# Attention's key and query loads: 12 transfers a tile with a repeated source, in place of 20

## The chip, the cores and the metric

The kernel is one program on one core of a Trainium2 chip. The metric is the device time of one execution in microseconds (us); less is better. Matmuls run on TensorE (PE in the profile, its weight loads PEld), the rest on VectorE (DVE), ScalarE (ACT) and GpSimd (POOL). The SyncE sequencer (SP) only issues transfers and waits. A transfer (DMA) can be issued by SP, ACT or POOL; its bytes are moved by the core's 16 DMA engines, in packets.

## The reference

Two transformer-like layers over a batch of 4 sequences of 512 rows of 256 numbers, all in float32. The part that the change touches is the causal attention of the first layer, with 16 heads of 16 numbers each:

```python
Q = split_heads(Xn @ Wq + bq)
K = split_heads(Xn @ Wk + bk)
V = split_heads(Xn @ Wv + bv)
scores = jnp.einsum('bhqd,bhkd->bhqk', Q, K) / jnp.sqrt(jnp.float32(D_HEAD))
scores = jnp.where(causal, scores, jnp.float32(-jnp.inf))
A = jax.nn.softmax(scores, axis=-1)
AV = jnp.einsum('bhqk,bhkd->bhqd', A, V)
return AV @ Wo + bo
```

After it come a mixture of 16 experts, a gated convolution with an MLP, and a mixture of 2 experts. None of them is touched.

## The kernel before

The program is a row of stages, each a block in which every engine has its own instruction stream, with semaphores between the streams and a barrier of all engines at each block's end.

**The projection stage** (`attention_inputs`) computes queries, keys and values for the four sequences b = 0 to 3 in a software pipeline (`wavefront`). Each float32 number is split into a high and a low part that TensorE can multiply exactly (`qhi` and `qlo`; names with k_parts, q_parts and v_parts are scratch tensors in device memory). SP stores the results with `store(b)`: for each b eight transfers of 256 KB at L212 (four to q_parts, four to k_parts) and one of 1 MB to v_parts at L216. The source of an L212 store is a tile of 128 partitions; its destination is seen as 8 blocks of 16 rows of 512 numbers, because the two parts of one head lie behind each other. ACT evicts the projections (L327), and in `first_keys` it also issues the very first key and query loads of attention, since SP is busy storing: half of them at b = 2 and half at b = 3. POOL makes `qlo` (L259), then the low part of V, and last stores five small row sets (L272, mod_rows), for whose arrival SP waits (L223) before the stage can end.

**The attention stage** (`attention`) works through 16 tiles, called quads below: 4 sequences times 4 groups of 4 heads. Its loop does two quads, u = 0 and u = 1, per turn (8 turns, a pair of quads each), and each has its own buffers: K4_0 and Q4_0, K4_1 and Q4_1. For head s of a quad, partitions 64·(s % 2) to 64·(s % 2) + 63 of the buffer hold the products' factors in this order: keys hi, lo, hi, lo against queries hi, lo, lo, hi, so that one matmul adds all four products. So every row is needed twice, and `load_keys` fetches it twice from device memory: for each head two transfers of 32 partitions for the keys (L560), one of 32 for the queries (L562) and two of 16 (L564). That is 20 transfers a quad. A row is 512 numbers, 2 KB.

PE computes the scores of a head (L660 with the mask at L661), DVE takes their maxima (L758), ACT the exponentials (L717), POOL scales (L635), PE transposes (L673), ACT and DVE split again (L727, L766), PE multiplies by V (L689), four heads behind the scores. SP's order in one turn of the loop, from `pair`: wait until the scores of quad u = 0 are done, then load_keys for the next quad in those buffers; the same for u = 1; wait until the values of u = 0 are done, then four loads of V (L568); the same for u = 1. PE waits at a quad's first matmul for all its K and Q transfers (`k_in`, `q_in`), and at its first value matmul for V.

Of the kernel before, what the change touches and what calls it, by code (L numbers as in the profile page):

```python
# [16 lines left out]
B, T = 4, 512  # L17
NT = B * T // P
TT = T // P
HEADS, DH = 16, 16  # L20
# [20 lines left out]
def f32(ap):  # L41

    return ap.bitcast(F32)
# [7 lines left out]
def wait(eng, sem, n):  # L51

    if not isinstance(n, int) or n > 0:
        eng.wait_ge(sem, n)

def wavefront(*stages):

    for step in range(B + max(lag for lag, _ in stages)):
        for lag, stage in stages:
            if 0 <= step - lag < B:  # L60
                stage(step - lag)
# [70 lines left out]
def attention_inputs(k, heads, x, cT, wmod, w, ln_gb, bqk, bv_row):  # L132
# [5 lines left out]
    with ExitStack() as c:  # L138
# [135 lines left out]
        @block.scalar  # L274
        def _(act):
            act.wait_ge(c_in, 16)
            act.activation(scT[:], cs[:], ACT.Silu).then_inc(silu_done, 1)

            def evict(b):

                if b < 2:
                    for i in (FIRST_LAYER[1:], SECOND_LAYER)[b]:
                        act.wait_ge(row_ready, i + 1)
                        act.activation(row[:, i, :], k.PS[0:B, 2 + i, :], ACT.Copy).then_inc(evicted, 1)
                    act.wait_ge(cols_ready, b + 1)
                    first, last = COL_PARTS[b][0], COL_PARTS[b][-1]
                    act.activation(k.modc[:, b, first:last + 1].rearrange("p c m b -> p (c m b)"),
                                   cols[:, b, DM * first:DM * (last + 1)].rearrange("p j b -> p (j b)"), ACT.Copy).then_inc(evicted, 1)

            def weights(b):  # L290
                if b == 0:
                    act.wait_ge(w_in, 48)
                    act.activation(whi[:], wst[:], ACT.Copy).then_inc(w_hi, 1)
                    act.wait_ge(par_in, 48)
                    act.mul(bq[:, 0], bq[:, 0], 0.25).then_inc(bq_done, 1)
                    act.wait_ge(bq_done, 1)

            def normalize(i, src, out, free, done):

                def stage(b):  # L300
                    act.wait_ge(nb_ready[i], b + 1)
                    free(b)
                    for t in range(TT):
                        act.activation(out(b, t), src(b, t), ACT.Identity, scale=rs[:, i, b, t:t + 1],
                                       bias=nb[:, i, b, t:t + 1]).then_inc(done, 1)
                return stage
            first_norm = normalize(0, lambda b, t: k.X[:, b * TT + t, :], lambda b, t: xh[:, b % 2, t, :],
                                   lambda b: wait(act, xh_used, b - 1), xh_done)
            second_norm = normalize(1, lambda b, t: h[:, b % 2, t, :], lambda b, t: hn[:, t, :],
                                    lambda b: wait(act, hT_ready, b * DM), hn_ready)  # L310

            def columns(b):

                if b >= 2:
                    act.wait_ge(v_ready, (b - 1) * 2)
                for m in range(DM):
                    act.wait_ge(hf_done, b * DM + m + 1)
                    act.activation(hhi[:, b % 2, m, :], k.PS[:, m, :], ACT.Identity, scale=gb[:, 0, m:m + 1],
                                   bias=gb[:, 1, m:m + 1]).then_inc(hhi_done, 1)

            def queries(j):
                def stage(b):
                    act.wait_ge(q_ready, b * 4 + j + 1)
                    if b:
                        act.wait_ge(q_out[j], b * 32)
                    for out in (qf[:, j, :], qhi[:, j, :]):
                        act.activation(out, k.PS[:, 2 + j, :], ACT.Identity, scale=(0.25 if j < 2 else 1.0),  # L327
                                       bias=bq[:, j // 2, j % 2:j % 2 + 1]).then_inc(q_done, 1)
                return stage

            def values(b):
                if b:
                    act.wait_ge(v_out, b * 16)
                for g in range(2):
                    act.wait_ge(vf_done, b * 2 + g + 1)
                    for t in (2 * g, 2 * g + 1):
                        last = act.activation(vp[:, t, :, 0, :], vf[:, t, :].rearrange("p (h d) -> p h d", d=DH), ACT.Copy)
                    last.then_inc(vhi_done, 1)

            def first_keys(b):  # L340

                if b >= 2:
                    act.wait_ge(heads.zeroed, 4)
                    heads.wait_stored(act, 0)
                    heads.load_keys(act, 0, 0, 0, range(2 * b - 4, 2 * b - 2))
            wavefront((2, columns), (3, queries(0)), (3, queries(1)), (3, queries(2)), (0, first_norm), (0, evict), (1, weights), (1, second_norm),
                      (3, queries(3)), (3, values), (3, first_keys))

        @block.vector
# [180 lines left out]
class Heads:  # L530
# [20 lines left out]
            pool.memset(f32(self.K4[u][:]), 0.0).then_inc(self.zeroed, 1)  # L551
            pool.memset(f32(self.V4[u][:]), 0.0).then_inc(self.zeroed, 1)

    def load_keys(self, sp, b, q, u, heads=range(4)):

        for s in heads:
            r = 64 * (s % 2)
            src = self.k.k_parts[b, q, s].rearrange("a r t -> (a r) t")
            for dup in range(2):
                sp.dma_start(f32(self.K4[u][r + 32 * dup:r + 32 * dup + 32, s, :]), src).then_inc(self.k_in[u], 16)  # L560
            src = self.k.q_parts[b, q, s]
            sp.dma_start(f32(self.Q4[u][r:r + 32, s // 2, :]), src.rearrange("a r t -> (a r) t")).then_inc(self.q_in[u], 16)  # L562
            for dup in range(2):
                sp.dma_start(f32(self.Q4[u][r + 32 + 16 * dup:r + 48 + 16 * dup, s // 2, :]), src[1 - dup]).then_inc(self.q_in[u], 16)  # L564

    def load_values(self, sp, b, q, u):
        for s in range(4):
# [14 lines left out]
def attention(k, heads, OT, out_weights, wo):  # L582
# [3 lines left out]
    with ExitStack() as c:  # L586
        Q4, K4, V4, k_in, q_in, v_in = heads.Q4, heads.K4, heads.V4, heads.k_in, heads.q_in, heads.v_in
# [58 lines left out]
        def _(pe):  # L646
            def body(it, on):
                for e in range(8):
                    h = it * 8 + e

                    def scores(i):
                        u, s = e // 4, e % 4
                        if s == 0 and i == 0:

                            pe.wait_ge(k_in[u], it * 128 + 128)
                            pe.wait_ge(q_in[u], it * 192 + 192)
                        w = P * (i + 1)

                        wait(pe, exp_done, (h - 1) * TT + i + 1)
                        pe.matmul(k.PS[:, i, 0:w], Q4[u][:, s // 2, P * i:P * i + P], K4[u][:, s, 0:w], start=True, stop=False)  # L660
                        pe.matmul(k.PS[:, i, w - P:w], k.identb[:], k.maskb[:], start=False, stop=True).then_inc(s_ready, 1)  # L661
# [31 lines left out]
                    if on(e, 0):  # L693
                        for i in range(TT - 1):
                            scores(i)
                    if on(e, VALUES):
                        values()
                    if on(e, 0):
                        scores(TT - 1)
# [1841 lines left out]
```

## Time and profile before

| | |
|---|---|
| median of 3 runs | 1178.86 us (1175.69 to 1179.64) |
| the profiled execution | 1173.97 us, span 1171.9 us |
| granted TensorE clock, mean over the span | 0.90 of full speed |
| PE busy | 954.3 us, 81% of the span |
| DVE, ACT, POOL busy | 742.1, 652.3, 456.9 us |
| attention stage, first score to last value | 118.4 to 362.2 us |
| bytes moved by DMA | 123.15 MB, mean 105 GB/s |

Times in a trace count from the start of the span. A timeline row gives start, duration, engine and line; a row with SPq, ACTq or POOLq is the issuing of a transfer by that sequencer, and its duration is how long the sequencer was held, not how long the bytes took. "To landing" is the time from issue to the last byte. The DMA share of a window is the mean busy share of the 16 DMA engines: 0.50 can be all of them half the time, or eight of them all the time.

### The profile page before, as it was taken

How to read it: one execution, taken by the hardware profiler on the slowest of the kernel's cores; microseconds unless marked ns; L12 is line 12 of the kernel's file. 1: busy time of each engine (PE TensorE's matmuls, PEld its weight loads, DVE VectorE, ACT ScalarE, POOL GpSimd, SP SyncE). 2: the span in 40 equal slices, each digit the busy share in tenths (PEclk: the TensorE clock that was granted, in tenths of full speed). 3: DMA queues.
4: the chain of work that ended last, by engine and by line, in shares of the span. 5: the costliest groups of instructions: out<-in, count | busy, mean ns of one | idle time of the engine just before them, and what ended most of it. 6: DMA issues, size and time to landing. Idle time of an engine off the chain costs nothing. (4 is left out here: it accounts for less than half of the span.)

```text
span 1171.9 us, 21496 instructions
## 1 busy us (share of the span) xinstructions
PE 954.3 (81%) x5454; PEld 796.3 (68%) x5454; DVE 742.1 (63%) x1917; ACT 652.3 (56%) x1693; POOL 456.9 (39%) x637
## 2 busy tenths in 40 slices
PE   6671999999997767969999970689699974999992
PEld 2461788888886655758999960468487753888882
DVE  4870798999994676468555535996447773444444
ACT  3562898999993345458666642579533322333331
POOL 3373564666662177603444443576301121010000
PEclk9786898999998787979999995799899986999997
DMA  7066443343322522447343429310042203000004
GB/s 247 17 222 212 114 102 90 91 90 90 90 54 64 180 100 101 153 150 251 124 128 121 126 98 303 99 45 1 14 143 75 72 28 127 24 31 33 28 15 152
DMA packets 112107, 123.15 MB, mean 105 GB/s; under 512 B 46720, under 2 KB 85120, under 8 KB 111896
## 3 DMA queue, kind: packets, MB, share of 16 engines
q1 hardware_dynamic: 102584, 97.89, 28.4%
q0 software_dynamic: 8608, 23.20, 5.3%
q10 hardware_dynamic: 832, 1.05, 0.3%
q8 instruction: 40, 0.66, 0.2%
q14 instruction: 43, 0.35, 0.1%
HBM read 77.73 MB, written 44.35 MB: 104 GB/s over the span
## 5 line engine op out<-in xcount | busy, mean ns | idle before, releaser
L717 ACT ACTIVATE PR<-PS,nmax 128x128 f32<-128x128 f32 (+3 forms) x256 | 135.7, 553 | 9.7 <-DVE nmax L758 8.4
L758 DVE TENSOR_REDUCE nmax<-PS 128x1 f32<-128x128 f32 (+3 forms) x256 | 113.5, 481 | 42.4 <-PE PS L661 37.0
L635 POOL TENSOR_SCALAR PR<-PR,rinv 128x128 f32<-128x128 f32 (+3 forms) x256 | 132.3, 537 | 0.0
L1355 POOL DMA_INDIRECT r_results<-r_y,r_to x79 | 75.9, 961 | 111.8 <-DVE r_to L1410 76.8
L660 PE MATMUL PS<-K,Q 128*128 128x128 f32 (+3 forms) x256 | 84.6, 390 | 30.4 <-PEq L138 26.4
L766 DVE TENSOR_TENSOR PTlo<-PS,PThi 128x512 fp32r<-128x512 f32 (+1 forms) x192 | 103.0, 590 | 2.9 <-ACT PThi L727 2.9
L727 ACT ACTIVATE PThi<-PS 128x512 fp32r<-128x512 f32 (+1 forms) x192 | 97.0, 547 | 6.7 <-PE PS L673 6.7
L673 PE MATMUL PS<-ident,PR 128*128 128x128 f32 x640 | 86.7, 281 | 3.6 <-DVE PTlo L766 3.0
L689 PE MATMUL PS<-PThi,V 128*128 128x512 f32 (+3 forms) x256 | 85.3, 346 | 1.1 <-DVE PTlo L766 0.5
L2350 DVE TENSOR_TENSOR x_h<-PS,x_sg 128x256 f32<-128x256 f32 x68 | 28.9, 424 | 86.4 <-ACT x_sg L2304 86.4
L2304 ACT ACTIVATE x_sg<-PS 128x256 f32<-128x256 f32 x68 | 26.2, 385 | 95.2 <-PE PS L2444 95.2
L2279 POOL DMA_INDIRECT x_results<-x_y,x_to x17 | 16.4, 963 | 156.2 <-DVE x_to L2345 143.8
L689 PE MATMUL PS<-PTlo,V 128*128 128x512 f32 (+3 forms) x256 | 76.2, 323 | 0.0
L673 PEld LDWEIGHTS PS<-ident,PR 128*128 128x128 f32 x640 | 69.6, 143 | 9.6 <-DVE PTlo L766 5.5
L949 POOL DMA_INDIRECT r_sorted<-o_hrow,o_slots x64 | 64.8, 1012 | 28.7 <-issue 18.7
L1399 DVE TENSOR_TENSOR r_xlo<-PS,r_xhi 128x256 fp32r<-128x256 f32 x79 | 33.4, 423 | 65.6 <-ACT r_xhi L1370 61.2
L660 PEld LDWEIGHTS PS<-K,Q 128*128 128x128 f32 x256 | 51.7, 206 | 32.8 <-issue 30.0
L2442 PE MATMUL PS<-r_wlo,r_xhi 128*128 x158 | 59.7, 378 | 2.5 <-issue 2.0
L1370 ACT ACTIVATE r_xhi<-PS 128x256 fp32r<-128x256 f32 x79 | 30.4, 385 | 56.1 <-PE PS L2444 54.0
L661 PE MATMUL PS<-maskb,identb 128*128 128x128 bf16 x256 | 60.8, 238 | 0.0
L717 ACT ACTIVATION_READ_ACCUMULATOR PR<-PS,nmax 128x1 f32 x256 | 58.7, 229 | 0.0
L2428 PE MATMUL PS<-x_w,x_hhi 128*128 (+1 forms) x136 | 57.2, 437 | 1.8 <-DVE x_hlo L2354 1.7
(374 smaller groups left out, 3067.8 us busy)
## 6 DMA issues: line engine op xcount, KB each, us to landing
r_xg<-r_sorted SPq DMA_DIRECT2D x79, 129.0 KB
r_wst<-in_routed SPq DMA_DIRECT2D x16, 608.0 KB, 5.3
K<-k_parts SPq DMA_DIRECT2D x120, 64.0 KB, 1.8
v_parts<-vp SPq DMA_DIRECT2D x4, 1024.0 KB, 7.5
V<-v_parts SPq DMA_DIRECT2D x64, 64.0 KB, 2.1
mlp_st<-r_results SPq DMA_DIRECT2D x8, 512.0 KB, 7.9
c_yg<-r_results SPq DMA_DIRECT2D x8, 512.0 KB
mlp_st<-in_up SPq DMA_DIRECT2D x8, 512.0 KB, 3.7
```

The costliest lines, as they stand in the source:

```text
L635: pool.tensor_scalar(PR[:, e % 4, i, 0:w], PR[:, e % 4, i, 0:w], rinv[:, e % 4, i:i + 1], 1.0, ALU.mult, ALU.mult).then_inc(norm_done, 1)
L660: pe.matmul(k.PS[:, i, 0:w], Q4[u][:, s // 2, P * i:P * i + P], K4[u][:, s, 0:w], start=True, stop=False)
L661: pe.matmul(k.PS[:, i, w - P:w], k.identb[:], k.maskb[:], start=False, stop=True).then_inc(s_ready, 1)
L673: ins = pe.transpose(k.PS[:, 4 + bank, at % 512:at % 512 + P], PR[:, (e - TRANS) % 4, i, P * j:P * j + P], k.ident[:])
L689: ins = pe.matmul(O[:, P * j:T], V4[u][:, j, s, :], pt[:, ge % 2, PT_AT[j]:PT_AT[j] + w], start=(s == 0 and j == 0 and part == 0), stop=(s ...
L717: act.activation(PR[:, e % 4, i, 0:w], k.PS[:, i, 0:w], ACT.Exp, bias=nmax[:, e % 4, i:i + 1], accum_out=rsum[:, e % 4, i:i + 1]).then_inc ...
L727: act.activation(PThi[:, e % 2, at:at + w], k.PS[:, 4 + n, 0:w], ACT.Copy).then_inc(hi_done, 1)
L758: dve.tensor_reduce(nmax[:, e % 4, i:i + 1], k.PS[:, i, 0:P * (i + 1)], AX_X, ALU.max, negate=True).then_inc(max_done, 1)
L766: dve.tensor_tensor(PTlo[:, (e - LO) % 2, at:at + w], k.PS[:, 4 + n, 0:w], f32(PThi[:, (e - LO) % 2, at:at + w]), ALU.subtract).then_inc(l ...
L949: pool.indirect_dma_start(out=d.sorted, out_offset=bass.IndirectOffsetOnAxis(ap=slots[:, b * TT + t, choice:choice + 1], axis=0), in_=hrow ...
L1355: pool.indirect_dma_start(out=d.results, out_offset=bass.IndirectOffsetOnAxis(ap=to[:, i % TO_LANES:i % TO_LANES + 1], axis=0), in_=y[:, i ...
L2442: pe.matmul(out, x_hi, w_lo, start=first, stop=False)
```

## The change

```diff
             def first_keys(b):
 
-                if b >= 2:
+                if b == 2:
                     act.wait_ge(heads.zeroed, 4)
                     heads.wait_stored(act, 0)
-                    heads.load_keys(act, 0, 0, 0, range(2 * b - 4, 2 * b - 2))
+                    heads.load_keys(act, 0, 0, 0)
...
-    def load_keys(self, sp, b, q, u, heads=range(4)):
-
-        for s in heads:
+    def load_keys(self, sp, b, q, u):
+
+
+        for s in range(4):
             r = 64 * (s % 2)
-            src = self.k.k_parts[b, q, s].rearrange("a r t -> (a r) t")
-            for dup in range(2):
-                sp.dma_start(f32(self.K4[u][r + 32 * dup:r + 32 * dup + 32, s, :]), src).then_inc(self.k_in[u], 16)
-            src = self.k.q_parts[b, q, s]
-            sp.dma_start(f32(self.Q4[u][r:r + 32, s // 2, :]), src.rearrange("a r t -> (a r) t")).then_inc(self.q_in[u], 16)
-            for dup in range(2):
-                sp.dma_start(f32(self.Q4[u][r + 32 + 16 * dup:r + 48 + 16 * dup, s // 2, :]), src[1 - dup]).then_inc(self.q_in[u], 16)
+            for a in range(2):
+                src = self.k.k_parts[b, q, s, a].unsqueeze(0).to_broadcast([2, DH, T])
+                sp.dma_start(f32(self.K4[u][r + 32 * a:r + 32 * a + 32, s, :]), src).then_inc(self.k_in[u], 16)
+            src = self.k.q_parts[b, q, s].rearrange("a r t -> (a r) t").unsqueeze(0).to_broadcast([2, 2 * DH, T])
+            sp.dma_start(f32(self.Q4[u][r:r + 64, s // 2, :]), src).then_inc(self.q_in[u], 16)
...
-                            pe.wait_ge(q_in[u], it * 192 + 192)
+                            pe.wait_ge(q_in[u], it * 64 + 64)
```

The keys now lie hi, hi, lo, lo and the queries hi, lo, hi, lo, which gives the same four products. A key transfer takes one part (16 rows) with its source repeated twice, in steps of (2, 16, 512) with a step of zero for the 2; a query transfer takes both parts (32 rows), repeated twice, in steps of (2, 32, 512). The bytes and the 2 KB rows moved are the same: 512 rows, 1 MB, a quad. A quad has 8 key transfers of 64 KB and 4 query transfers of 128 KB, 12 in place of 20.

On SP, at the start of the attention stage, the second quad's keys and queries and the first two quads' values stand like this before the change (shapes are those of the destination; the number behind a name is the buffer u):

```order
L560 DMA K4_1<-k_parts 32x512 x2
L562 DMA Q4_1<-q_parts 32x512
L564 DMA Q4_1<-q_parts 16x512 x2
L560 DMA K4_1<-k_parts 32x512 x2
L562 DMA Q4_1<-q_parts 32x512
L564 DMA Q4_1<-q_parts 16x512 x2
L568 DMA V4_0<-v_parts 128x4x32 x4
L568 DMA V4_1<-v_parts 128x4x32 x4
```

These are its last two heads of four; the first two read alike. After the change the same place reads:

```order
L561 DMA K4_1<-k_parts 32x1x512 x2
L563 DMA Q4_1<-q_parts 64x1x512
L561 DMA K4_1<-k_parts 32x1x512 x2
L563 DMA Q4_1<-q_parts 64x1x512
L567 DMA V4_0<-v_parts 128x4x32 x4
L567 DMA V4_1<-v_parts 128x4x32 x4
```

The place in SP's order is the same; three issues a head stand where five stood.

On ACT, in the projection stage, the loads for the first quad stood in two batches, one behind the evictions of b = 2 and one behind those of b = 3 (L327 are evictions of queries and keys, L337 of values):

```order
L337 ACTIVATE vp<-vf 128x16x16 x4
L560 DMA K4_0<-k_parts 32x512 x2
L562 DMA Q4_0<-q_parts 32x512
L564 DMA Q4_0<-q_parts 16x512 x2
L560 DMA K4_0<-k_parts 32x512 x2
L562 DMA Q4_0<-q_parts 32x512
L564 DMA Q4_0<-q_parts 16x512 x2
L327 ACTIVATE qf<-PS,bq 128x512
```

Now all twelve stand in front of the evictions of b = 3:

```order
L337 ACTIVATE vp<-vf 128x16x16 x4
L561 DMA K4_0<-k_parts 32x1x512 x2
L563 DMA Q4_0<-q_parts 64x1x512
L561 DMA K4_0<-k_parts 32x1x512 x2
L563 DMA Q4_0<-q_parts 64x1x512
L561 DMA K4_0<-k_parts 32x1x512 x2
L563 DMA Q4_0<-q_parts 64x1x512
L561 DMA K4_0<-k_parts 32x1x512 x2
L563 DMA Q4_0<-q_parts 64x1x512
L327 ACTIVATE qf<-PS,bq 128x512
```

Ten transfers stood ahead of these evictions before, twelve do now, and the ten behind them are gone. The order of the other engines is unchanged.

## Rows read from the trace of the kernel before

**Rows 1.** The page's first line.

```profile
span 1171.9 us, 21496 instructions
```

**Rows 2.** Windows: first quad, fifth quad, quads 7 to 15.

```profile
core 0: us, PE busy (x) PEld busy (x) DVE busy (x) ACT busy (x) POOL busy (x), PEclk, DMA share, GB/s
118.37:131.29 12.92, 11.59 (x52) 8.77 (x53) 8.76 (x22) 11.03 (x35) 4.66 (x12) 0.61 0.47 119
177.09:193.53 16.44, 16.44 (x105) 14.39 (x105) 13.04 (x32) 12.19 (x39) 6.88 (x17) 0.82 0.32 76
208.30:337.21 128.91, 127.49 (x937) 109.66 (x937) 124.26 (x298) 124.65 (x404) 79.99 (x180) 1.00 0.39 91
```

**Rows 3.** Waits of PE, 131 to 355 us: total, times, longest.

```profile
PE PS L660 <- DMA Q<-q_parts: 2.9, 1, 2.9
```

**Rows 4.** Timeline of PE: first score of quads 7 and 16.

```profile
208.30 0.32 PE L660 MATMUL PS<-K,Q 128*128 128x128 f32 x1 [0.15 <-ACT PR L717]
...
337.21 0.31 PE L660 MATMUL PS<-K,Q 128*128 128x128 f32 x1
```

**Rows 5.** DMA issues by tile: count, KB each, median us to landing.

```profile
K<-k_parts SPq DMA_DIRECT2D x120, 64.0 KB, 1.8
...
V<-v_parts SPq DMA_DIRECT2D x64, 64.0 KB, 2.1
...
Q<-q_parts SPq DMA_DIRECT2D x60, 64.0 KB
Q<-q_parts SPq DMA_DIRECT2D x120, 32.0 KB
```

**Rows 6.** Windows in the projection stage: L212 stores alone, then the v_parts store.

```profile
73.00:76.80 3.80, 0.74 (x6) 0.74 (x7) 3.51 (x6) 1.29 (x4) 1.37 (x2) 1.00 0.53 198
96.00:98.00 2.00, 0.00 (x0) 0.00 (x0) 0.00 (x0) 0.00 (x0) 0.00 (x0) 0.50 1.01 329
```

**Rows 7.** DMA, 72 to 76.5 us: queue (packets, MB, share), then issues.

```profile
q1 hardware_dynamic: 450, 0.87, 52.7%
...
k_parts<-qhi SPq DMA_DIRECT2D x2, 256.0 KB
k_parts<-qlo SPq DMA_DIRECT2D x2, 256.0 KB
```

**Rows 8.** Timeline of SP: two L212 stores.

```profile
68.44 0.61 SPq L212 DMA_DIRECT2D q_parts<-qhi  x1
...
73.02 1.31 SPq L212 DMA_DIRECT2D k_parts<-qlo  x1
```

**Rows 9.** Timeline of ACT: its loads behind b = 2, and what follows.

```profile
84.75 0.40 ACTq L560 DMA_DIRECT2D K<-k_parts  x1
...
96.22 3.07 ACTq L564 DMA_DIRECT2D Q<-q_parts  x2
99.40 0.69 ACT L327 ACTIVATE qf<-PS,bq 128x512 f32<-128x512 f32 x1 [13.39 <-issue]
```

**Rows 10.** Timeline of POOL: the row sets' issue; their landing.

```profile
108.40 2.85 POOL L272 DMA_DIRECT2D mod_rows<-row  x5
...
DMA to landing us min/median/max: 5.5/6.8/6.9
```

**Rows 11.** Timeline of SP: values, then output weights.

```profile
128.53 5.51 SPq L568 DMA_DIRECT2D V<-v_parts  x8
...
160.67 4.73 SPq L579 DMA_DIRECT2D wo_st<-in_wo  x8
```

**Rows 12.** DMA queue, 129.5 to 134.5 us (values), 161 to 166 us (output weights).

```profile
q1 hardware_dynamic: 3696, 0.46, 59.4%
...
q1 hardware_dynamic: 1324, 0.55, 49.0%
```

## The prediction

> **What bounds the kernel now.** I started from the page's first line, the span of 1171.9 us [rows 1], and cut it at the attention stage, the only long stage that the change touches. In its steady part PE is busy 127.5 of 128.9 us at full clock (the third window of [rows 2]). From quad 7's first score to quad 16's are 337.21 - 208.30 = 128.9 us, nine quads of 14.3 us each [rows 4]. The reader is to see that PE, with DVE and ACT right behind it at 124 us, sets the pace, and that the DMA engines stand at a share of 0.39 and 91 GB/s. Then I read PE's waits in this stage. Transfers of K and Q held it up once, for 2.9 us, at quad 5, where the loads of the output weights had put SP behind [rows 3]. So the key and query loads are hidden, and fewer issues have nothing to shorten here. The question is whether the loads stay hidden.
>
> **How a transfer's shape sets its speed.** I then looked at the stores of the projection stage, since there transfers queue up and the engines' limit shows. The L212 stores read 128 partitions and write 8 blocks of 16 rows. While they alone are under way, the 16 DMA engines show a share of 0.53 and 198 GB/s (the first window of [rows 6]; [rows 7] shows that nothing else was issued). This is no lack of work: SP is held 1.31 us by one such store, where an earlier one with a free queue took 0.61 us [rows 8]. The v_parts store, whose outermost step counts 128 on both sides, reaches a share of 1.01 and 329 GB/s (the second window of [rows 6]). I read this so: a transfer is cut along the outermost step of its access on both sides, and the side with the fewer steps limits how many engines work on it. Eight blocks give eight engines, and always the same eight, or the next store in the queue would have filled the others. One engine then moves 198 / 8 = 24.8 GB/s, a 2 KB row in 83 ns.
>
> The old key and query transfers are flat: 32 or 16 rows on both sides, so 16 engines with one or two rows each. The new sources begin with the repetition, an outermost step of 2. By the same reading each new transfer goes over two engines, and all of them over the same two.
>
> The page "DMA: Bandwidth & Descriptors" of the Trainium skill says this outright (Rules for kernel authors, "Use all 16 engines"): an outermost dimension of size c below 16, a leading zero-stride broadcast among its examples, confines the whole DMA to at most c engines. By that rule the eight-block stores should show a share of 0.50; the trace agrees, with 0.53. The same section has a rule for the change: coalesce many small transfers, since those under 64 KB are mostly overhead. By it the time would fall or stay, and the trace is against that having anything to give, as the wait of 2.9 us says.
>
> **The change in the attention stage.** A quad's keys and queries are 8 x 64 + 4 x 64 + 8 x 32 = 1024 KB before (the counts of [rows 5] over 15 quads) and as many after: 1.049 MB / (2 x 24.8 GB/s) = **21.2 us** on the two engines, against 14.3 us of computing. The eight value loads of a pair of quads lie in the same queue. They keep an engine busy 59.4% of 5 us = 3.0 us at least [rows 12], and SP's issuing takes 5.5 us at most [rows 11]; I take the middle, 4.3 us. So a pair of quads needs 2 x 21.2 + 4.3 = **46.7 us**, where it took 28.6 us. The queue is rarely empty: the next loads into buffer 0 may start once the scores of quad u = 0 are done, which is 21.2 + 1 + 14.3 = 36.5 us into the period of 46.7 us, and those into buffer 1 about 11 us in, when the queue gets to them at 21.2 us. The cover is 10 us both times. TensorE's clock does not change that. Waiting PE will be at half clock more often, but the fifth quad, at a mean of 0.82, took 16.4 us (the second window of [rows 2]). That is 2.1 us more for (1 - 0.82) x 2 x 16.4 = 5.9 us at half clock, so about 14.3 + 5.1 = 19.4 us for a quad at half clock throughout, within the cover. The 8 issues a quad that are saved are worth nothing against this, nor is the wait of 2.9 us that goes with them.
>
> **The change in the projection stage.** ACT's ten loads took from 84.75 to 99.3 us to issue, at about 1.45 us each, because SP's stores were queued; the evictions of b = 3 waited 13.4 us behind them [rows 9]. From their start at 99.4 us the rest of the chain follows: POOL's work, its row sets from 108.4 us (2.85 us to issue, 6.8 us to land [rows 10]), and the end of the stage at about 118.2 us, 18.8 us later. After the change the two engines have, from 84 us on, SP's 13 remaining L212 stores (16 rows per engine each), two v_parts stores (32 each) and the first quad's 256: 208 + 64 + 256 = 528 rows, 528 x 83 ns = 43.8 us, so until 127.8 us. The evictions start when most of ACT's 256 and SP's 112 rows of b = 2 are through, at about 110 us, which also gives 110 + 19 = 129 us. I take **129 us** for the start of attention. The ends: 118.2 us if the queues swallow all without holding ACT, 134 us if ACT is held to its last row.
>
> **The sum.** Quad 2's loads and the first values: 129 + 21.2 + 4.3 = 154.5 us. Seven pairs of 46.7 us: 481.4 us. The output weights, once, between 2.5 us (49% of 5 us [rows 12]) and 4.7 us [rows 11], say 3.0: 484.4 us. The last values come behind the last keys: - 4.3. One us for landing (a key load takes 1.8 us from issue to landing with nothing ahead [rows 5]): quad 16 starts at 481.1 us, where it started at 337.2 us [rows 4]: + 143.9 us. The last quad and the tail begin at less than full clock, between 0 and 5 us, I take 2. In all **+146 us**. The profiled execution took 1173.97 us, so 1320 us; on the median of 1178.86 us it would be 1325 us. I give **1318 us**, a shade under both, since 198 GB/s is the slowest I saw eight engines run when full and has a moment of slack in it. Nothing behind attention is changed.
>
> The ends of the unknown costs: start at 118.2 us, values 3.0 us, weights 2.5 us, no tail give 1297 us, and engines 5% faster take another 16 us off, 1281 us. Each engine at 329 / 16 = 20.6 GB/s, as in the v_parts store, with every other term at its high end, would be 25.5 us a quad and about 1400 us; but there all 16 were drawing on device memory at once, two will not. One engine at 22.8 GB/s, halfway, gives about 1350 us.
>
> **The rivals.** *All 16 engines serve the new transfers anyway* (chance 0.10): the eight blocks are on the written side and come from distinct rows, and a repeated read may be cut differently. Then the loads stay hidden, SP issues 8 transfers a quad less, PE's 2.9 us at quad 5 go, and ACT's twelve issues in place of ten ahead of the evictions cost 2 x 1.45 = 2.9 us: between 1170 and 1177 us on the profiled time, no change. This is the case on the other side, not slower. It decides from four engines on: 10.6 us of loads and 2.2 of values are then under the 14.3 us of a quad. The rule to coalesce belongs here, with a chance of a third of it for a gain over the bound. *Two engines each, but others from transfer to transfer* (0.04): SP would issue faster than two engines move, and eight pairs would work side by side; same time as the first rival. Against it stands the half share under a full queue. *Four engines or so* (0.04), if the inner step of 16 or 32 takes part: hidden in attention, a few us lost in the projection stage, 1180 to 1190 us. The forecast, two fixed engines, has 0.82.
>
> **How the numbers follow.** A difference of 0.3%, 3.5 us, is about what a measurement of this kernel can tell from none. Faster: 0.03, a third of the first rival. Same: the rest of it and the second, 0.11. Slower: 0.82 + 0.04 = 0.86. The range is the forecast's own, 1280 to 1350 us; the other cases, 0.18 in all, lie below it.
>
> **What would show it.** If right: in the steady part of attention the DMA share is about 2/16 = 0.13 plus a little for the values, with 60 GB/s or less; K and Q loads land many us after issue in place of 1.8; SP is held over 1 us by an issue where it took 0.37; PE's first score of each quad waits about 9 us for K or Q; quads start every 23.4 us; the clock falls in the waits; POOL's L272 issues at about 119 us. It is wrong if key loads still land in 2 to 3 us with a share near 0.4, or if PE's waits sit elsewhere.

## The result, and the profile after

The changed kernel takes 1340.2 us (median of 4 runs, 1337.11 to 1340.75) against 1177.28 us before: the ratio is 1.1382, with a 95% interval of 1.1344 to 1.142. That is 163 us more, where 139 were forecast (1318 us, range 1280 to 1350).

The page of the changed kernel, its first line and three of its lists (compare [rows 1] and [rows 5]; the queue row gives packets, MB and share):

```profile
span 1338.7 us, 21262 instructions
...
q1 hardware_dynamic: 98144, 97.87, 23.8%
...
L659 PE MATMUL PS<-K,Q 128*128 128x128 f32 (+3 forms) x256 | 95.7, 432 | 165.6 <-DMA Q<-q_parts 113.7
...
K<-k_parts SPq DMA_DIRECT2D x120, 64.0 KB
Q<-q_parts SPq DMA_DIRECT2D x60, 128.0 KB
V<-v_parts SPq DMA_DIRECT2D x64, 64.0 KB, 2.2
```

Queue 1 moves the 97.9 MB that it moved before, but PE's score matmuls at L659 (L660 before) now have 165.6 us of idle time in front of them, 113.7 of it put down to the query loads.

PE's waits in the changed kernel, 131 to 513 us (compare [rows 3]):

```profile
PE PS L659 <- DMA Q<-q_parts: 113.7, 14, 14.9
PE PS L659 <- issue: 13.7, 1, 13.7
```

One wait of 2.9 us has become a wait at every quad. The same place by windows: nine quads of the steady part, and ten of its microseconds in which only key and query rows are moved (compare [rows 2]):

```profile
core 0: us, PE busy (x) PEld busy (x) DVE busy (x) ACT busy (x) POOL busy (x), PEclk, DMA share, GB/s
283.47:498.27 214.80, 146.67 (x936) 126.44 (x937) 128.33 (x297) 130.44 (x405) 79.88 (x180) 0.80 0.19 55
335.00:345.00 10.00, 10.00 (x77) 8.87 (x76) 8.90 (x22) 8.13 (x26) 5.61 (x14) 0.97 0.13 49
```

Nine quads take 214.8 us in place of 128.9. The reader is to see the second window: a DMA share of 0.13, with 49 GB/s. Sixteen times 0.13 is two engines, busy all the time. This is no idle queue, as the timeline of SP shows in the same stretch:

```profile
331.35 3.66 SPq L561 DMA_DIRECT2D K<-k_parts  x2
335.14 1.12 SPq L563 DMA_DIRECT2D Q<-q_parts  x1
336.56 4.13 SPq L561 DMA_DIRECT2D K<-k_parts  x2
340.79 1.16 SPq L563 DMA_DIRECT2D Q<-q_parts  x1
342.14 5.14 SPq L567 DMA_DIRECT2D V<-v_parts  x2
```

SP is held in its issues, and so are the two value loads behind them, 2.6 us each, though they go over all engines. Over all 64 value loads of each kernel (ns min/median/max; L568 is before, L567 after):

```profile
L568 SPq DMA_DIRECT2D V<-v_parts x64: 368/373/1732, 128.5 to 337.9; - x64
L567 SPq DMA_DIRECT2D V<-v_parts x64: 372/1606/2607, 145.7 to 499.1; - x64
```

The projection stage, ACT and POOL (compare [rows 9, 10]), and the first scores of quads 1, 2 and 16 (compare [rows 4]):

```profile
92.28 7.22 ACTq L561 DMA_DIRECT2D K<-k_parts  x2
...
108.84 1.24 ACTq L563 DMA_DIRECT2D Q<-q_parts  x1
110.20 0.69 ACT L327 ACTIVATE qf<-PS,bq 128x512 f32<-128x512 f32 x1 [23.57 <-issue]
...
119.20 2.85 POOL L272 DMA_DIRECT2D mod_rows<-row  x5
...
129.95 0.44 PE L659 MATMUL PS<-K,Q 128*128 128x128 f32 x1 [37.77 <-PEq L138]
...
157.10 0.44 PE L659 MATMUL PS<-K,Q 128*128 128x128 f32 x1 [13.74 <-issue]
...
498.27 0.47 PE L659 MATMUL PS<-K,Q 128*128 128x128 f32 x1 [5.10 <-DMA Q<-q_parts]
```

The evictions of b = 3 begin at 110.2 us, where they began at 99.4, and attention at 129.95 us, where it began at 118.4. Quad 16 begins 161.1 us later than before.

### The profile page after: what moved, and what is told of

Its sections match the earlier page's. It is cut to its first block and busy times, and to the rows that moved or that the text cites. A ratio compares the mean times of both kernels' runs of the same rounds, so it can differ in the third digit from the quotient of the medians.

```text
span 1338.7 us, 21262 instructions
## 1 busy us (share of the span) xinstructions
PE 985.6 (74%) x5454; PEld 822.7 (61%) x5454; DVE 747.2 (56%) x1917; ACT 659.6 (49%) x1693; POOL 456.0 (34%) x637
## 3 DMA queue, kind: packets, MB, share of 16 engines
q10 hardware_dynamic: 536, 1.05, 0.2%
## 5 line engine op out<-in xcount | busy, mean ns | idle before, releaser
L757 DVE TENSOR_REDUCE nmax<-PS 128x1 f32<-128x128 f32 (+3 forms) x256 | 118.1, 485 | 199.0 <-PE PS L660 193.2
L659 PE MATMUL PS<-K,Q 128*128 128x128 f32 (+3 forms) x256 | 95.7, 432 | 165.6 <-DMA Q<-q_parts 113.7
L659 PEld LDWEIGHTS PS<-K,Q 128*128 128x128 f32 x256 | 59.4, 235 | 169.8 <-issue 169.1
L631 POOL TENSOR_TENSOR carry<-rinv 128x1 f32<-128x1 f32 x64 | 12.4, 193 | 255.9 <-DVE rinv L783 255.8
L688 PE MATMUL PS<-PThi,V 128*128 128x512 f32 (+3 forms) x256 | 96.2, 386 | 1.0 <-DVE PTlo L765 0.5
L688 PE MATMUL PS<-PTlo,V 128*128 128x512 f32 (+3 forms) x256 | 85.7, 360 | 0.0
L672 PEld LDWEIGHTS PS<-ident,PR 128*128 128x128 f32 x640 | 74.8, 151 | 4.6 <-issue 0.9
L660 PE MATMUL PS<-maskb,identb 128*128 128x128 bf16 x256 | 65.9, 258 | 0.0
L688 PEld LDWEIGHTS PS<-PThi,V 128*128 128x128 f32 x256 | 57.6, 225 | 5.0 <-DVE PTlo L765 0.7
L688 PEld LDWEIGHTS PS<-PTlo,V 128*128 128x128 f32 x256 | 56.8, 222 | 3.5
```

Of the source, the lines that this page charges most:

```text
L672: ins = pe.transpose(k.PS[:, 4 + bank, at % 512:at % 512 + P], PR[:, (e - TRANS) % 4, i, P * j:P * j + P], k.ident[:])
L688: ins = pe.matmul(O[:, P * j:T], V4[u][:, j, s, :], pt[:, ge % 2, PT_AT[j]:PT_AT[j] + w], start=(s == 0 and j == 0 and part == 0), stop=(s ...
L757: dve.tensor_reduce(nmax[:, e % 4, i:i + 1], k.PS[:, i, 0:P * (i + 1)], AX_X, ALU.max, negate=True).then_inc(max_done, 1)
```

## The experiments

The theory is that of the prediction: the outermost step of a transfer's access, on either side, limits the engines that work on it, and an outermost step of 2 leaves the same two. The rivals: the repeated read itself is slow, or the larger and fewer transfers are; and for the projection stage, the moved issues rather than the slow transfers delay it. Each expectation was written before its run. The kernel before was run again beside each group. The code below leaves out the lines that only adapt PE's counts of arrived transfers; "..." marks other gaps.

### e1: the repetition inside

```diff
-            for a in range(2):
-                src = self.k.k_parts[b, q, s, a].unsqueeze(0).to_broadcast([2, DH, T])
-                sp.dma_start(f32(self.K4[u][r + 32 * a:r + 32 * a + 32, s, :]), src).then_inc(self.k_in[u], 16)
-            src = self.k.q_parts[b, q, s].rearrange("a r t -> (a r) t").unsqueeze(0).to_broadcast([2, 2 * DH, T])
-            sp.dma_start(f32(self.Q4[u][r:r + 64, s // 2, :]), src).then_inc(self.q_in[u], 16)
+            src = self.k.k_parts[b, q, s].rearrange("a r t -> (a r) t").unsqueeze(1).to_broadcast([2 * DH, 2, T])
+            sp.dma_start(f32(self.K4[u][r:r + 64, s, :]), src).then_inc(self.k_in[u], 16)
+            for a in range(2):
+                src = self.k.q_parts[b, q, s].rearrange("a r t -> r a t")
+                sp.dma_start(f32(self.Q4[u][r + 32 * a:r + 32 * a + 32, s // 2, :]), src).then_inc(self.q_in[u], 16)
```

> Twelve transfers a quad as in the change, with the source repeated and the same 1 MB, but the repetition is an inner step: one key transfer of 64 partitions per head with steps (32, 2, 512), the 2 with a stride of zero, and two query transfers of 32 partitions with steps (16, 2, 512). Theory (the outermost step of 2 leaves two engines): 16 engines work again, loads are hidden; PE's wait of 2.9 us goes and ACT issues 12 in place of 10 ahead of the evictions (+2.9 us), so 1174 to 1181 us against 1177. Rival (the repeated read, or fewer and larger transfers, is what is slow): about 1340 us as the change.

ACT's loads of the first quad stand at b = 2, as in the change. Measured: 1173.8 us, the kernel before beside it 1174.9; ratio 0.9995 (0.998 to 1.001). Windows of e1, nine quads:

```profile
204.50:333.40 128.90, 127.48 (x936) 109.63 (x937) 124.33 (x298) 124.54 (x404) 79.47 (x180) 1.00 0.37 92
```

The steady part takes 128.9 us again, with a share of 0.37. Twelve transfers, a repeated source for the keys, the same bytes: none of them is slow. Not only the place of the 2 differs from the change: the keys now come in one transfer of 64 rows a head, and the queries in two of 32 rows that repeat nothing inside a transfer. e2 tests the step by itself.

### e2: an outermost step of 2 with nothing repeated

```diff
-        self.q_parts = dram("q_parts", [B, QUADS, 4, 2, DH, T])
-        self.k_parts = dram("k_parts", [B, QUADS, 4, 2, DH, T])
+        self.q_parts = dram("q_parts", [B, QUADS, 4, 2, DH + 1, T])[:, :, :, :, 0:DH]
+        self.k_parts = dram("k_parts", [B, QUADS, 4, 2, DH + 1, T])[:, :, :, :, 0:DH]
...
-            src = self.k.k_parts[b, q, s].rearrange("a r t -> (a r) t")
+            src = self.k.k_parts[b, q, s]
```

The first query transfer's source is left unflattened in the same way.

> The kernel before with its 20 transfers a quad and nothing repeated inside a transfer; the scratch tensors get an unused 17th row behind each part, so that the 12 transfers of 32 rows can't be flattened and have steps (2, 16, 512) at the source. Theory: these 12 go over two engines with 16 rows each, and with 8 more rows of the 16-row ones that is 200 rows a quad on the busiest engines; at the change's 84.6 ns a row 16.9 us a quad, 38.6 us a pair with the values: about 1260 us (1245 to 1280). Rival (the repeated read is what is slow): 1177 us, same as before.

Measured: 1258.5 us, ratio 1.0717 (1.0686 to 1.0747). The kernel before, with one unused row behind each part in device memory, is 84 us slower. DMA queue of e2, 270 to 280 us, and its windows over nine quads:

```profile
GB/s 49 90 123 74 123 74 49 49 57 49 57 49 49 49 66 148 66 139 49 41 49 49 49 49 49 49 49 57 156 49 148 66 49 49 49 49 49 49 49 49
```

```profile
248.50:418.40 169.90, 137.86 (x937) 118.43 (x937) 126.72 (x297) 127.32 (x401) 78.75 (x179) 0.89 0.25 69
```

The first row is 40 slices of a quarter microsecond. Its floor is the change's 49 GB/s (some slices 41, as there); I read the peaks as the transfers of 16 rows that still go over all engines. The pair of quads takes 37.8 us (169.9 / 4.5) where 38.6 were worked out. So the slowness needs no repetition; the outermost step of 2 suffices. The changed pitch of the scratch rows does not explain it either, since the rate falls to that of two engines and no other.

### e3, e10 and e11: the queries alone

e3 has the change's query transfer; its keys come flat, 16 rows at a time. Against the change:

```diff
-            for a in range(2):
-                src = self.k.k_parts[b, q, s, a].unsqueeze(0).to_broadcast([2, DH, T])
-                sp.dma_start(f32(self.K4[u][r + 32 * a:r + 32 * a + 32, s, :]), src).then_inc(self.k_in[u], 16)
+            for a in range(2):
+                for dup in range(2):
+                    at = r + 32 * a + 16 * dup
+                    sp.dma_start(f32(self.K4[u][at:at + 16, s, :]), self.k.k_parts[b, q, s, a]).then_inc(self.k_in[u], 16)
```

(ACT's first loads stand in two batches, as in the kernel before.)

> The change's repeated transfer for the queries alone; the keys come flat, in 16 transfers of 16 rows a quad, so 20 in all. Theory: 128 rows a quad on the two engines plus 16 of the keys, 144 rows x 84.6 ns = 12.2 us, with the values 29.2 us a pair against the 28.6 us of computing: just about hidden, so 1177 to 1195 us with a few us of it in the projection stage. Rival (a cost that goes with the bytes so loaded): half of the loss of 163 us, about 1258 us.

Measured: 1224.6 us, ratio 1.0425 (1.0394 to 1.0456). Neither number was right: 50 us are lost where at most 18 were expected and the rival said 83. Waits of PE in e3, 131 to 400 us, and the first score of one quad:

```profile
PE PS L659 <- DMA Q<-q_parts: 35.5, 7, 8.7
```

```profile
267.82 0.32 PE L659 MATMUL PS<-K,Q 128*128 128x128 f32 x1 [4.65 <-DMA Q<-q_parts]
```

PE waits at every second quad. SP issued that quad's first key load at 250.31 us, 17.5 us before this score, and PE had run out of work at 267.82 - 4.65 = 263.2 us, 12.9 us after that issue. The sum of work, 29 us a pair, had left out that a buffer's loads can't start before its scores are done, so that only the other buffer's work covers them. Here that work would have covered 15.6 us, since the last score on the buffer ended at 247.6 us. SP, however, issued the other quad's four value loads first:

```profile
247.54 2.04 SPq L567 DMA_DIRECT2D V<-v_parts  x4
250.31 1.78 SPq L561 DMA_DIRECT2D K<-k_parts  x4
```

So 12.9 us were left, and of the wait of 4.65 us the 2.7 us from 247.6 to 250.3 come from SP's order. The order is that of the kernel before; keys ahead of these values, which would be the obvious remedy, was not run. To see whether the time from first issue to last landing can be shortened, e10 issues the four query transfers ahead of the sixteen key transfers:

```diff
         for s in heads:
             r = 64 * (s % 2)
+            src = self.k.q_parts[b, q, s].rearrange("a r t -> (a r) t").unsqueeze(0).to_broadcast([2, 2 * DH, T])
+            sp.dma_start(f32(self.Q4[u][r:r + 64, s // 2, :]), src).then_inc(self.q_in[u], 16)
+        for s in heads:
+            r = 64 * (s % 2)
...
-            src = self.k.q_parts[b, q, s].rearrange("a r t -> (a r) t").unsqueeze(0).to_broadcast([2, 2 * DH, T])
-            sp.dma_start(f32(self.Q4[u][r:r + 64, s // 2, :]), src).then_inc(self.q_in[u], 16)
```

> e3 (repeated transfers of outermost step 2 for the queries alone, 1224.6 us) with the four query transfers issued ahead of the quad's sixteen key transfers. Rows, engines and the number of issues are the same. Theory (what counts in e3 is not the queue's average load of 29 us a pair but the time from the first issue of a quad's loads, once its buffers are free, to the last landing, against the 14.3 us that the other quad's scores cover; the queries, last in each head, land about 17.5 us after it): now the two engines start about 1.5 us earlier and never run dry between heads, so the last query lands about 14 us in, and most of PE's wait of 4 us at every second quad goes: 1185 to 1205 us. Rival (e3 is bound by the sum of work, on the two engines or in SP's issues): unchanged, 1222 to 1227 us.

> e3 once more beside e10 on the same chip, as its yardstick: 1222 to 1227 us.

Measured: e10 1224.7 us, e3 beside it 1224.2 us. No gain; the expectation fell. Timeline of SP and PE in e10, and PE's waits, 131 to 400 us:

```profile
283.53 2.71 SPq L559 DMA_DIRECT2D Q<-q_parts  x4
286.35 4.93 SPq L565 DMA_DIRECT2D K<-k_parts  x9
...
300.46 0.32 PE L661 MATMUL PS<-K,Q 128*128 128x128 f32 x1 [3.62 <-DMA K<-k_parts]
```

```profile
PE PS L661 <- DMA K<-k_parts: 34.8, 8, 7.7
```

From first issue to first score are 16.9 us, hardly less than 17.5, and PE now waits for the keys. Each of the sixteen key transfers has one row on each of the two engines, and these now stand behind the queries' 128. The order within the queue only names another transfer as the last one. The 144 rows are 12.2 us of work for an engine; what the rest of the 16.9 us is was not taken apart.

e11 takes rows off the two engines: two of the four heads' queries come flat. Against e3:

```diff
-            src = self.k.q_parts[b, q, s].rearrange("a r t -> (a r) t").unsqueeze(0).to_broadcast([2, 2 * DH, T])
-            sp.dma_start(f32(self.Q4[u][r:r + 64, s // 2, :]), src).then_inc(self.q_in[u], 16)
+            src = self.k.q_parts[b, q, s].rearrange("a r t -> (a r) t")
+            if s % 2:
+                for dup in range(2):
+                    sp.dma_start(f32(self.Q4[u][r + 32 * dup:r + 32 * dup + 32, s // 2, :]), src).then_inc(self.q_in[u], 16)
+            else:
+                sp.dma_start(f32(self.Q4[u][r:r + 64, s // 2, :]), src.unsqueeze(0).to_broadcast([2, 2 * DH, T])).then_inc(self.q_in[u], 16)
```

> As e3, but only two of a quad's four query transfers have the outermost step of 2; the other two heads' queries come in two flat transfers of 32 rows each. 22 transfers a quad, the same rows. The two engines have 64 + 16 + 8 = 88 rows a quad, 7.4 us, in place of 144 rows, 12.2 us. Theory (the time from the first issue to the last landing, 17 to 17.6 us in e3 and e10 made of 12.2 us on the two engines and about 5 us of issue and landing, is set against the 14 us that the other quad's scores cover): it falls to 12 or 13 us and is hidden, PE's waits of about 4 us at every second quad go to nothing, and the time falls to 1174 to 1182 us. Rival (a cost in proportion to the rows on the two engines, as for a queue that is always busy): half of e3's loss of 50 us, about 1200 us.

Measured: 1187.5 us, ratio 1.0114 (1.0087 to 1.0141), 14.6 us above the kernel before, between the two expectations. PE's waits in e11, 131 to 365 us:

```profile
PE PS L663 <- DMA Q<-q_parts: 11.3, 6, 5.9
```

The steady part decides. Quads 7 to 16 start 128.9 us apart before, 152.8 us in e3 and 131.1 us in e11: with half of the query rows on the two engines the loss over nine quads falls from 23.9 to 2.2 us, not to half. That speaks for a cover which is or is not exceeded. In e11 a quad of buffer 0 has its first key load issued at 232.60 us and its first score at 246.99 us, 14.4 us later where the expectation said 12 or 13, and PE had waited 1.53 us: 14.4 us against a cover of 12.9 us, as 17.5 against 12.9 gave a wait of 4.65 us in e3. Quad 7 itself starts 8.8 us later than before (217.1 for 208.3 us): attention begins 4.1 us later, the wait at quad 5 is 5.9 us in place of 2.9, and the rest was not taken apart.

### e5 and e7: the moved issues, with the old loads

e5 is the kernel before with `if b == 2` and all 20 transfers there; e7 the same with `if b == 3`.

> The kernel before, with all 20 old transfers of the first quad at b = 2 on ACT: the reordering alone. Theory (ACT is held by SP's queued stores and, in the change, by the two engines' full queues): the first ten take 14.6 us as before, the next ten find SP idle and take about 0.5 us each, so the evictions of b = 3 start some 5 us later: about 1182 us. Rival (the delay of 11.6 us of the attention stage's start in the change came from moving the issues, not from the two engines): 1188 to 1192 us.

> The kernel before with its old 20 transfers of the first quad all on ACT behind the evictions of b = 3: the same move as e6 without the new transfers. Theory: the same start of the evictions, but 20 issues among SP's last stores last until about 118 us, so the first scores wait a little: 1167 to 1175 us. If e6 and e7 are alike, the gain is the move's, and nothing of it the larger transfers'.

Measured: e5 1177.9 us, ratio 1.0033 (1.0015 to 1.0052); e7 1177.5 us, ratio 1.0031 (1.0014 to 1.0047). Timeline of ACT in e5:

```profile
102.51 0.69 ACT L327 ACTIVATE qf<-PS,bq 128x512 f32<-128x512 f32 x1 [16.23 <-issue]
```

The evictions start 3.1 us later than before and attention 2.7 us later. e5 stayed under the 1182 us expected, because the first ten issues took 12 us in place of 14.6. e1 has the change's twelve issues in the same place, without the slow transfers, and its attention starts 2.0 us later than before (120.4 us). So of the change's 11.6 us in this stage 2 to 3 come from moving the issues, and the rest from the slow transfers.

e7 missed its 1167 to 1175 us. Its evictions of b = 3 did start early, at 88.2 us, but ACT's twenty issues lasted until 117.7 us, and the stage ended at 118.1 us, where it ended at 118.2 us before.

### e6, e8, e9 and e12: a version that beats both

e6 is e1 with `if b == 3`. e8 has `if b == 2` again and changes the scratch layout, so that the stores have one outermost step of 128; its loads, 16 a quad, replace those of the change:

```diff
-        self.q_parts = dram("q_parts", [B, QUADS, 4, 2, DH, T])
-        self.k_parts = dram("k_parts", [B, QUADS, 4, 2, DH, T])
+        self.q_parts = dram("q_parts", [B, QUADS, 4, DH, 2, T])
+        self.k_parts = dram("k_parts", [B, QUADS, 4, DH, 2, T])
...
-                        sp.dma_start(dst[b, 2 * (j % 2):2 * (j % 2) + 2, :, part].rearrange("q s r t -> (q s) r t"),
+                        sp.dma_start(dst[b, 2 * (j % 2):2 * (j % 2) + 2, :, :, part].rearrange("q s r t -> (q s r) t"),
...
+            for a in range(2):
+                part = slice(r + 32 * a, r + 32 * a + 32)
+                src = self.k.k_parts[b, q, s, :, a].unsqueeze(1).to_broadcast([DH, 2, T])
+                sp.dma_start(f32(self.K4[u][part, s, :]), src).then_inc(self.k_in[u], 16)
+                src = self.k.q_parts[b, q, s].rearrange("r a t -> (r a) t")
+                sp.dma_start(f32(self.Q4[u][part, s // 2, :]), src).then_inc(self.q_in[u], 16)
```

e9 is e8 with `if b == 3`. e12 is e9 with `out_weights.load(sp, wo)` behind SP's loop in place of ahead of it.

> e1 (twelve transfers, repetition as an inner step) with ACT's first loads behind the evictions of b = 3 in place of ahead of them. Theory (in the kernel before, the evictions of b = 3 wait for ACT's issues, and the attention stage starts 19 to 21 us after they do): the evictions start at about 93 us in place of 101, attention at about 112 to 114 us in place of 120, and the first quad's loads have landed by then: 1165 to 1170 us. Rival (the row sets or SP's stores set the stage's end, or the first quad's loads now come late): 1173 us or more, like e1.

> The scratch tensors hold the high and low part of a row side by side, so that the L212 stores have one outermost step of 128 on both sides in place of 8; the loads are 16 a quad (keys with steps (16, 2, 512), the 2 repeated; queries flat), ACT's all at b = 2. Theory (the outermost step sets the engines on the store's side too): a store keeps near 16 engines busy, with a DMA share near 1 where it was 0.53, SP is held about 0.7 us a store, ACT's 16 issues are not held by it, and the evictions of b = 3 start earlier than in e1: 1165 to 1173 us. Rival (stores of 8 blocks are slow for another reason, such as writing device memory): share stays near 0.5 and the time at 1174 to 1178 us.

> e8 with ACT's first loads behind the evictions of b = 3. Theory: the gains of e6 and e8 overlap, since both take the same hold away: 1162 to 1169 us, at or a little under e6.

> e9 with SP's load of the output weights behind the attention loop in place of behind the second pair of quads. Theory (in e9 PE waits 4.0 us for keys at quad 5, because SP issues the weights' eight transfers, 4.7 us, ahead of them): that wait goes, 1162 to 1164 us, and the weights land well before the next stage needs them. Rival (the wait at quad 5 is for the projection stage's last stores, or the weights then come late): 1166 to 1168 us, as e9.

| kernel | us | ratio to before (95%) | attention starts at |
|---|---|---|---|
| e6 | 1173.2 | 0.999 (0.9979 to 1.0002) | 120.3 us |
| e8 | 1170.5 | 0.9962 (0.9949 to 0.9975) | 112.5 us |
| e9 | 1166.7 | 0.9935 (0.9918 to 0.9953) | 108.5 us |
| e12 | 1161.6 | 0.9895 (0.9879 to 0.9912) | 108.4 us |

e6 missed. Its evictions of b = 3 did start at 90.0 us, but ACT's twelve issues now lay among SP's last stores and were held by them:

```profile
103.34 0.65 ACTq L560 DMA_DIRECT2D K<-k_parts  x1
...
116.84 1.26 ACTq L563 DMA_DIRECT2D Q<-q_parts  x2
118.78 1.28 ACT L716 ACT_TABLE_LOAD   x1 [14.32 <-PEq L138]
```

They ended at 118.1 us, the stage's barrier opened at 118.8, and PE's first score waited for these loads until 120.3 us. The hold had moved, not gone. e8 changes the stores that hold: DMA of e8, 70 to 72 us, in which the four stores shown were issued (compare [rows 6, 7, 8]), and one store in SP's timeline:

```profile
q1 hardware_dynamic: 419, 0.76, 103.0%
...
q_parts<-qhi SPq DMA_DIRECT2D x1, 256.0 KB, 2.2
q_parts<-qlo SPq DMA_DIRECT2D x1, 256.0 KB, 2.5
k_parts<-qhi SPq DMA_DIRECT2D x1, 256.0 KB, 2.0
k_parts<-qlo SPq DMA_DIRECT2D x1, 256.0 KB, 2.4
```

```profile
71.67 0.45 SPq L212 DMA_DIRECT2D k_parts<-qlo  x1
```

Stores of the same bytes keep all 16 engines busy, at 380 GB/s (0.76 MB in 2 us) in place of 198, and SP is held 0.45 us in place of 1.31. e9 adds the move that had nothing to give in e6, and its span is 4.0 us shorter than e8's (1163.5 for 1167.5 us). PE's waits in e9, 110 to 360 us, still have this row:

```profile
PE PS L660 <- DMA Q<-q_parts: 4.0, 1, 4.0
```

In e12 PE waits for no key or query load between 110 and 360 us, and the span is another 4.0 us shorter, 1159.5 us. e12 is 11.3 us, 1%, faster than the kernel before beside it (1172.9 us).

## Why the prediction was right

**The two engines.** Right, and shown from several sides: the share of 0.13 in the changed kernel, e1 with the repetition inside (no loss), e2 with the step and no repetition (84 us), and e8, where the store's eight blocks become one step of 128 and the half share a full one. That it is always the same two engines is read from the floor of 49 GB/s with SP held; the trace names no engine.

The page "DMA: Bandwidth & Descriptors" of the Trainium skill (Rules for kernel authors, "Use all 16 engines") gives the rule, that a short outermost dimension confines a transfer to as many engines, with a broadcast as its example; the trace agrees, with 0.13 for a step of 2. The other rule of that section of the Trainium skill, to coalesce transfers below 64 KB, found nothing to gain here: e1 has 12 in place of 20 at the same time.

**The rate.** 198 GB/s over eight engines gave 83 ns for a row. The windows of [rows 6] were a good guide: 49 GB/s over two is 84 ns, and keys and queries of a quad took 21.7 us (quad 7's first score to quad 8's) for 21.2 forecast. To set 1318 us below the sums of 1320 and 1325 us, in the hope of a faster rate, was wrong by a little: the rate was the slower one.

**A pair of quads.** 46.7 us were forecast. From quad 2 to quad 16 are 498.3 - 157.1 = 341.2 us, less 4.2 for the output weights, for seven pairs: 48.1 us each, which makes 10 us of the miss. Two thirds of it is the rate (2 x 0.5 us). The rest is the value loads: SP is held in them, and the two engines then stand without key rows for a moment. Window 353 to 357 us of the changed kernel, between them:

```profile
353.00:357.00 4.00, 3.17 (x12) 2.69 (x12) 2.23 (x5) 1.69 (x6) 0.00 (x0) 0.50 0.48 76
```

Its share of 0.48 is that of values; SP issues keys again at 355.35 us, and for half a microsecond, from 356.3 us, nothing moves at all. "The queue is rarely empty" was nearly right.

**The projection stage.** 129 us forecast, 129.95 measured, and the evictions at 110.2 for 110. The forecast read this off the rows on the engines, and e1 and e5 fit it: without the slow transfers one batch costs only 2 to 3 us.

**Quad 2.** Of the single terms this one was mis-sized most, though the 1.4 us of a pair, seven times over, weigh more in the sum. It was to start at 129 + 21.2 + 1 = 151.2 us and started at 157.1. The sum had taken the queues as empty at 129 us. They were not: the last v_parts store, issued at 122.94 us, took 12.6 us to landing, so until 135.5 us, and the windows show more than the 49 GB/s of the two engines still moving behind 130 us (the store's issue row first, then the windows).

```profile
v_parts<-vp SPq DMA_DIRECT2D x1, 1024.0 KB, 12.6
...
124.00:130.00 6.00, 0.05 (x1) 0.08 (x1) 0.00 (x0) 0.24 (x1) 0.00 (x0) 0.50 0.75 253
130.00:136.00 6.00, 5.91 (x22) 4.06 (x22) 4.37 (x11) 5.35 (x16) 1.52 (x4) 0.50 0.19 68
```

The kernel before had shown the same: its last v_parts store, issued at 111.83 us, landed at 122.0 us, 3.8 us into the attention stage.

**The rest.** The output weights cost 4.2 us for 3.0. From quad 16's first score to the end of the span are 840.4 us for 834.7 before: 5.7 us for the 2 forecast. In the traces of the other runs the same stretch takes 836.0 to 840.1 us, whatever their loads (838.1 us in e1, whose steady part is as before), so most of the 5.7 us is not shown to be the loads'. Together: quad 16 17.2 us later than forecast, 3.7 us behind it, 21 us on the trace's own sum of 1320 us.

**The cover.** The clock did fall in the waits, to a mean of 0.80, and did not count, as forecast: every quad still waited 4.9 us or more for its queries. The price of the clock was worked out wrongly, though. If 5.9 us at half clock cost 2.1 us, a quad all at half clock takes 14.3 / (1 - 2.1 / 5.9) = 22.2 us and not 19.4, which is 7.9 us more and still within 10. But the cover of 10 us that the forecast gave itself was judged by a queue that is always full. e3 shows the other limit, which the forecast did not have: with less work in the queue it is the time of one quad's loads from first issue to last landing, 17.5 us, against what is left of one quad of computing when SP comes to issue them, 12.9 us. At the rival "four engines or so" this limit might have decided; that case was not run.

## What to carry to other kernels

Before merging transfers or repeating a source, write down the outermost step of both sides: it limits how many DMA engines work on the transfer (shown here for 2 and 8), and a repetition belongs inside, behind the rows. A transfer that is hidden has nothing to give in issue time, but it can lose its cover, and it is covered only if its time from first issue to last landing fits between the moment its buffer comes free and the moment it is needed; the sum over a period is not enough. What the issuing sequencer does between the two, such as other loads ahead of these, eats from the cover. A DMA share of k/16 that stays flat while the issuing sequencer is held is the sign to look for, in stores as in loads.

## What the runs showed of the hardware that was not expected

Transfers queued on a few engines hold what is issued behind them, on another sequencer too. In the changed kernel value loads that go over all 16 engines took a median of 1.6 us to issue, and 2.6 us at most, in place of 0.37 us. In e6 ACT's twelve issues took 14.8 us, 1.2 us each, during and behind SP's stores of eight blocks, though each had only 2 or 4 rows for an engine. In e9, at the same place with stores over all engines, sixteen took 12.9 us, 0.8 us each. ACT's transfers are in a queue of their own in the trace (q10, 1.05 MB, which is the first quad), so a full queue of SP's does not say why ACT is held; that was not shown.
